# Three PSUM banks for the gates and the inverse root's tiny operations spread between mixing and candidate, in a two-layer graph network kernel

## What is computed

```python
h = jnp.maximum(_layernorm(x, axis=-1), 0.0)
x = x + _L0_gnn_ref(h, ...)          # messages, segment_sum, then the GRU update:
#   r = sigmoid(i_r + h_r);  z = sigmoid(i_z + h_z)
#   n = tanh(i_n + r * h_n); new = (1 - z) * n + z * h
h = jnp.maximum(_layernorm(x, axis=-1), 0.0)
x = x + _L1_gnn_ref(h, edge_index, edge_attr_16, ...)
#   starts from projections of h: h @ W_att1 (source and target parts)
```

## Time and profile before

| | |
|---|---|
| median of 3 runs | 7310.7 us (7306.98 to 7316.62) |
| profiled execution, its own time | 7319.67 us |
| its span | 7317.9 us |
| update of layer 0 within it | 2479 to 2741 us |
| busy over the span: TensorE, VectorE, ScalarE, GpSimd | 77%, 61%, 29%, 68% |

### The profile page before, as it was taken

One profiled execution on the slowest core, in us unless ns is written; L12 is line 12 of the kernel. 1 busy time (PEld: TensorE's weight loads), 2 busy tenths in 40 slices (PEclk: granted clock), 3 DMA queues, 4 the chain that ended last, 5 costly groups with the idle time before them and its releaser, 6 DMA issues.

```text
span 7317.9 us, 186920 instructions
## 1 busy us (share of the span) xinstructions
PE 5607.2 (77%) x34843; PEld 4551.4 (62%) x34844; DVE 4494.2 (61%) x19972; ACT 2133.7 (29%) x6161; POOL 5006.6 (68%) x10349
## 2 busy tenths in 40 slices
PE   5555777878655767888788888886888888888885
PEld 2345555555555547777777777775767666666773
DVE  3466777777433663333333333333999999999997
ACT  3111100000000242222222222222555555555553
POOL 0377777777777356777777777776777777777771
PEclk8755565555555686666666656666898999999889
DMA  7223322222322123333333333333333333333332
GB/s 218 76 57 59 59 57 56 58 57 56 57 58 58 41 80 127 106 107 107 103 102 102 103 101 102 102 102 131 91 95 94 95 95 94 94 95 94 94 91 72
DMA packets 1128092, 649.01 MB, mean 89 GB/s; under 512 B 782033, under 2 KB 1031683, under 8 KB 1127044
## 3 DMA queue, kind: packets, MB, share of 16 engines
q1 hardware_dynamic: 766708, 357.79, 19.4%
q0 software_dynamic: 137728, 233.30, 10.5%
q10 hardware_dynamic: 223584, 57.12, 3.4%
HBM read 360.62 MB, written 311.42 MB: 92 GB/s over the span
## 4 chain that ended last, share of the span: by engine, by line
PE 20%; issue 16%; POOL 11%; DVE 9%; ACT 2%; DMA 2%; DVEq 1%; POOLq 1%; ACTq 0%; SPq 0%
PE banks L1287 9%; PE banks L1289 6%; POOL rows_by_src L779 4%; DVE h L1836 2%; PE banks L1334 2%; DMA rows_by_src<-ring 2%; PE banks L1288 2%; DVE h L1841 1%; DVE ring L1847 1%; PE banks L1275 1%; ACT ring L995 1%; POOL ring L840 1%; POOL ring L824 1%; DVE acc L1832 1%; POOL ring L821 1%
## 5 line engine op out<-in xcount | busy, mean ns | idle before, releaser
L779 POOL DMA_INDIRECT rows_by_src<-ring x1760 | 1779.5, 1011 | 563.7 <-issue 496.1
L751 POOL DMA_INDIRECT wide<-msg_table,ring x1664 | 1629.6, 979 | 761.9 <-issue 451.9
L1287 PE MATMUL banks<-wide,ring 128*128 x3520 | 1240.3, 450 | 271.5 <-ACT ring L988 183.3
L1287 PEld LDWEIGHTS banks<-wide,ring 128*128 128x128 f32 x3520 | 818.1, 286 | 352.0 <-issue 349.8
L1289 PE MATMUL banks<-h,ring 128*128 x3520 | 964.6, 371 | 0.0
L1289 PEld LDWEIGHTS banks<-h,ring 128*128 128x128 f32 x3520 | 837.2, 292 | 123.1
L995 ACT COPY ring<-banks 128x416 f32<-128x416 f32 x880 | 402.3, 510 | 1651.2 <-PE banks L1289 1651.2
L1204 PE MATMUL banks<-wide,ring 128*128 x3520 | 813.9, 412 | 66.1 <-DVE ring L1683 64.2
L1204 PEld LDWEIGHTS banks<-wide,ring 128*128 128x128 f32 x3520 | 779.9, 323 | 127.2 <-issue 123.2
L1804 DVE COPY ring<-ring 128x4 f32<-128x4 f32 x440 | 80.4, 183 | 1229.6 <-DMA rows_by_src<-ring 1229.4
L1169 PE MATMUL banks<-ident,ring 128*128 128x128 f32 x1248 | 421.1, 467 | 534.7 <-ACT ring L926 289.0
(11 more groups left out here) (317 smaller groups left out, 10757.3 us busy)
## 6 DMA issues: line engine op xcount, KB each, us to landing
h<-rows_by_src SPq DMA_DIRECT2D x1776, 105.0 KB, 2.0
ring<-attr_turned SPq DMA_DIRECT2D x440, 128.0 KB, 2.3
attr_turned<-ring ACTq DMA_DIRECT2D x416, 96.0 KB
rows_by_src<-ring POOLq DMA_INDIRECT x1760, 2.5
wide<-msg_table,ring POOLq DMA_INDIRECT x1664
msg_table<-ring SPq DMA_DIRECT2D x100, 256.0 KB, 2.0
ring<-attr_by_dst SPq DMA_DIRECT2D x208, 64.0 KB
attr_turned<-ring ACTq DMA_DIRECT2D x208, 64.0 KB
```

Source lines behind the costliest of these rows:

```text
L751: g.indirect_dma_start(out=A_g[:, b * GV + u, :], out_offset=None, in_=table[:, :], in_offset=bass.IndirectOffsetOnAxis(ap=A_idx[:, s, u:u ...
L779: g.indirect_dma_start(out=rows_d[:, :], out_offset=bass.IndirectOffsetOnAxis(ap=B_pos[:, s, u:u + 1], axis=0), in_=B_row[:, s, u, :], in_ ...
L1287: mm(b[:, 0:H1], B_DT[:, t, u, :], q_tab[:, w, :].rearrange("p a k -> p (a k)"), start=True, stop=False)
```

## The change

- The gates of pair j go to bank 2, 3 or 7 in turn (`G_BANK`), and TensorE waits for the sum of pair j-3 instead of j-2. Bank 7 is not used by anything else in this stage. `G_t` keeps two buffers, with ScalarE's wait on them.
- The inverse root of group g no longer stands in one block in slot 5g+8. Its twelve operations are called one at a time by `root(k, n_of_slot)`, six in slot 5g+9 and six in slot 5g+10: one behind each of the four operations of mixing and adding and the two of the candidate. Each waits for its own predecessor by `s_std`, which now counts operations. A dependent operation of mixing waits for its predecessor (`ch.need`) behind the tiny one.
- The deviation (5g+6), the square (5g+7) and the sum of squares (5g+8) keep their slots. The scaling moves from slot 5g+9 to 5g+11, which is the slot of the next group's deviation, and stands behind it. `G_LAG` grows from 11 to 13 and `G_STORE` with it: all that follows the scaling (TensorE's turns and products, ScalarE's copies, GpSimd's parts, SP's stores) comes two slots later.

The number of instructions is the same on every engine.

```diff
--- before.py
+++ after.py
@@ -79,8 +79,9 @@
 AT_SQRT, AT_FLAG, AT_COUNTS, AT_SORT, AT_TURN, AT_BOUND = 7, 13, 16, 19, (22, 24), (27, 30, 32)
 G_GROUP = 5
 N_GROUPS = NW // 2 // G_GROUP
-G_NORM = (G_GROUP + 1, G_GROUP + 2, G_GROUP + 3, G_GROUP + 4)
-G_LAG = 2 * G_GROUP + 1
+G_DEV, G_SQ, G_VAR, G_ROOT, G_SCALE = (G_GROUP + n for n in (1, 2, 3, 4, 6))
+G_LAG = 2 * G_GROUP + 3
+G_BANK = (2, 3, 7)
 G_SLOTS = NW // 2 + G_LAG + 2
 G_STORE = G_LAG + 5
 RSQRT_BITS = 0x5f3759df
@@ -951,13 +952,13 @@
                     act.wait_ge(g_mm, j + 1)
                     if j >= 2:
                         act.wait_ge(g_x, j - 1)
-                    a.activation(G_t[:, j % 2, :, :], two(bank[2 + j % 2], 4 * HID)[:, :, HID:GATES], ACT.Tanh, scale=0.5).then_inc(g_t, 1)
+                    a.activation(G_t[:, j % 2, :, :], two(bank[G_BANK[j % 3]], 4 * HID)[:, :, HID:GATES], ACT.Tanh, scale=0.5).then_inc(g_t, 1)
                 if k == T + 1:
                     act.wait_ge(r_pos, R_STEP * RANK_LOOPS)
                     a.copy(recs1[:, :, 0], src_T).then_inc(r_c, 1)
                     a.copy(recs1[:, :, 1], place_T).then_inc(r_c, 1)
                     act.wait_ge(r_c, 2 * REC0)
-                g, step = divmod(k - G_NORM[1], G_GROUP)
+                g, step = divmod(k - G_SQ, G_GROUP)
                 if 0 <= g < N_GROUPS and step == 0:
                     act.wait_ge(s_dev, g + 1)
                     if g >= 2:
@@ -1238,10 +1239,10 @@
                 if 0 <= j < T:
                     pe.wait_ge(g_Tc, j + 1)
                     pe.wait_ge(c_in[j % H_SLOTS], X_LOADS[j % H_SLOTS] + 16 * (j // H_SLOTS + 1))
-                    if j >= 2:
-                        pe.wait_ge(g_x, j - 1)
+                    if j >= 3:
+                        pe.wait_ge(g_x, j - 2)
                     for u in range(2):
-                        b = bank[2 + j % 2][:, u * 4 * HID:(u + 1) * 4 * HID]
+                        b = bank[G_BANK[j % 3]][:, u * 4 * HID:(u + 1) * 4 * HID]
                         mm(b, ones_b[:, :], bias3[:, 0:BIAS0], start=True, stop=False)
                         last = mm(b, h0m[:, j % H_SLOTS, u, :], wst0[:, :], start=False, stop=True)
                     last.then_inc(g_mm, 1)
@@ -1735,47 +1736,83 @@
             for t in P_hT:
                 v.memset(t[HID:HID + 1, :, :], 1.0).then_inc(p_ones, 1)
 
-            def norm_group(g, step):
-
-                n = 2 * G_GROUP
+            n = 2 * G_GROUP
+
+            def of_group(g):
                 w = slice(g * n, (g + 1) * n)
-                var, std, total = (small[:, j * NW + w.start:j * NW + w.stop] for j in range(3))
+                return (w,) + tuple(small[:, j * NW + w.start:j * NW + w.stop] for j in range(3))
+
+            def spread(g):
+
+                w, _, _, total = of_group(g)
+                dve.wait_ge(g_x, (g + 1) * G_GROUP)
+                ch.link(v.tensor_reduce(total, xs[:, w, :], AX.X, ALU.add))
+                v.scalar_tensor_tensor(h[:, w, :], per_row(total, n), -1.0 / HID, xs[:, w, :], ALU.mult, ALU.add).then_inc(s_dev, 1)
+
+            def root(k, n_of_slot):
+
+                g, late = divmod(k - G_ROOT, G_GROUP)
+                if not (0 <= g < N_GROUPS and late < 2):
+                    return
+                _, var, std, t = of_group(g)
+                step = 6 * late + n_of_slot
+                dve.wait_ge(s_std, 2 + 12 * g + step) if step else dve.wait_ge(s_var, 2 + g + 1)
                 if step == 0:
-                    ch.link(v.tensor_reduce(total, xs[:, w, :], AX.X, ALU.add))
-                    v.scalar_tensor_tensor(h[:, w, :], per_row(total, n), -1.0 / HID, xs[:, w, :], ALU.mult, ALU.add).then_inc(s_dev, 1)
-                if step == 2:
-                    dve.wait_ge(s_sq, g + 1)
-                    v.tensor_reduce(var, G_sq[:, g % 2, :, :], AX.X, ALU.add).then_inc(s_var, 1)
-                    dve.wait_ge(s_var, 2 + g + 1)
-                    ch.link(v.tensor_scalar(var, var, 1.0 / HID, EPS, ALU.mult, ALU.add))
-                    ch.link(v.tensor_scalar(std.bitcast(i32), var.bitcast(i32), 1, None, ALU.arith_shift_right))
-                    ch.link(v.tensor_scalar(std.bitcast(i32), std.bitcast(i32), -1.0, float(RSQRT_BITS), ALU.mult, ALU.add))
-                    for turn_no in range(3):
-                        ch.link(v.scalar_tensor_tensor(total, std, -0.5, var, ALU.mult, ALU.mult))
-                        ch.link(v.tensor_tensor(total, total, std, ALU.mult))
-                        m = v.scalar_tensor_tensor(std, total, 1.5, std, ALU.add, ALU.mult)
-                        if turn_no < 2:
-                            ch.link(m)
-                    m.then_inc(s_std, 1)
-                if step == 3:
-                    dve.wait_ge(s_std, 2 + g + 1)
-                    v.scalar_tensor_tensor(h[:, w, :], h[:, w, :], 0.0, per_row(std, n), ALU.max, ALU.mult).then_inc(s_h, 1)
+                    m = v.tensor_scalar(var, var, 1.0 / HID, EPS, ALU.mult, ALU.add)
+                elif step == 1:
+                    m = v.tensor_scalar(std.bitcast(i32), var.bitcast(i32), 1, None, ALU.arith_shift_right)
+                elif step == 2:
+                    m = v.tensor_scalar(std.bitcast(i32), std.bitcast(i32), -1.0, float(RSQRT_BITS), ALU.mult, ALU.add)
+                elif step % 3 == 0:
+                    m = v.scalar_tensor_tensor(t, std, -0.5, var, ALU.mult, ALU.mult)
+                elif step % 3 == 1:
+                    m = v.tensor_tensor(t, t, std, ALU.mult)
+                else:
+                    m = v.scalar_tensor_tensor(std, t, 1.5, std, ALU.add, ALU.mult)
+                m.then_inc(s_std, 1)
 
             T = NW // 2
             for k in range(G_SLOTS):
-                if 1 <= k < T + 1:
-                    j = k - 1
-                    w = slice(2 * j, 2 * j + 2)
-                    mix(j // G_PAIRS, j % G_PAIRS, h[:, w, :], g_n)
-                    v.tensor_tensor(xs[:, w, :], xs[:, w, :], G_d[:, j % 2, :, :], ALU.add).then_inc(g_x, 1)
+                j = k - 1
+                w, old, d, e = slice(2 * j, 2 * j + 2), G_n[:, j % 2, :, :], G_d[:, j % 2, :, :], G_e[:, j % 2, :, :]
+                if 0 <= j < T:
+                    dve.wait_ge(g_n, j + 1)
+                    m = ch.do(v.tensor_tensor(d, h[:, w, :], old, ALU.subtract))
+                root(k, 0)
+                if 0 <= j < T:
+                    ch.need(m)
+                    m = ch.do(v.scalar_tensor_tensor(e, G_t[:, j % 2, :, HID:2 * HID], 1.0, d, ALU.add, ALU.mult))
+                root(k, 1)
+                if 0 <= j < T:
+                    ch.need(m)
+                    m = ch.do(v.scalar_tensor_tensor(d, e, 0.5, old, ALU.mult, ALU.add))
+                root(k, 2)
+                if 0 <= j < T:
+                    ch.need(m)
+                    v.tensor_tensor(xs[:, w, :], xs[:, w, :], d, ALU.add).then_inc(g_x, 1)
+                root(k, 3)
                 if k < T:
-                    candidate(k // G_PAIRS, k % G_PAIRS, two(bank[2 + k % 2], 4 * HID), g_t, g_v)
-                for step, lag in enumerate(G_NORM):
-                    g, rest = divmod(k - lag, G_GROUP)
-                    if 0 <= g < N_GROUPS and rest == 0:
-                        if step == 0:
-                            dve.wait_ge(g_x, (g + 1) * G_GROUP)
-                        norm_group(g, step)
+                    gates, u = two(bank[G_BANK[k % 3]], 4 * HID), G_u[:, k % 2, :, :]
+                    dve.wait_ge(g_t, k + 1)
+                    m = ch.do(v.scalar_tensor_tensor(u, G_t[:, k % 2, :, 0:HID], 1.0, gates[:, :, GATES:4 * HID], ALU.add, ALU.mult))
+                root(k, 4)
+                if k < T:
+                    ch.need(m)
+                    v.scalar_tensor_tensor(G_v[:, k % 2, :, :], u, 0.5, gates[:, :, 0:HID], ALU.mult, ALU.add).then_inc(g_v, 1)
+                root(k, 5)
+                g, rest = divmod(k - G_DEV, G_GROUP)
+                if 0 <= g < N_GROUPS and rest == 0:
+                    spread(g)
+                g, rest = divmod(k - G_VAR, G_GROUP)
+                if 0 <= g < N_GROUPS and rest == 0:
+                    dve.wait_ge(s_sq, g + 1)
+                    v.tensor_reduce(of_group(g)[1], G_sq[:, g % 2, :, :], AX.X, ALU.add).then_inc(s_var, 1)
+                g, rest = divmod(k - G_SCALE, G_GROUP)
+                if 0 <= g < N_GROUPS and rest == 0:
+                    w, _, std, _ = of_group(g)
+                    dve.wait_ge(s_std, 2 + 12 * (g + 1))
+                    v.scalar_tensor_tensor(h[:, w, :], h[:, w, :], 0.0, per_row(std, n), ALU.max, ALU.mult).then_inc(s_h, 1)
+
 
             dve.wait_ge(r_c, 2 * REC0)
             v.memset(B_row[:, :, :, ROW_ONE:ROW], 1.0).then_inc(b_pad, 1)
```

## The result

The changed kernel took 7274.77 us (median of five, 7271.24 to 7281.26), the kernel before beside it 7311.99 us (five, 7306.98 to 7318.92): 0.9948 times, 95% interval 0.9934 to 0.9961. That is 38 us less by the ratio, 28 to 48. The forecast was 7278.6, within 7263 to 7298. A second series gave 7274.31 against 7310.41, 0.995 (0.9936 to 0.9964).

The account below looks back on a forecast made before the run. No engine was full: VectorE, TensorE and ScalarE waited in a ring in layer 0's update. Terms of -4.6 us per steady group made -37.4 in all, +5.4 for the lag, net -32: 7278.6 us, range 7263 to 7298.

Parts of the forecast that it names:

- The block (-4.03): VectorE, layer 0's update: the twelve tiny operations no longer stand in a row, saving 4.03 us per steady group.
- its return (+1.0): Tiny operations spread over two VectorE slots beside GpSimd still cost 1.0 us per group, bounds 0.2 to 1.9.
- Rival 2: VectorE: nothing hides the spread tiny operations, 3.2 us per group instead of 1.0; kernel 7296 us; chance 0.12.
- The wait behind the scaling (-2.1): VectorE's wait for the candidate's tanh shrinks from 2.47 us (1.84 to 2.78) to 0.38 per group.
- the tanh wait that the scaling had hidden (+0.38): VectorE: moving the scaling saves 0.73 us per group but uncovers a tanh wait of 0.38.
- Mixing beside GpSimd (+1.3): GpSimd's chain falls on VectorE mixings formerly free of it: +1.0 us in one slot, +0.3 in another, per group.
- The third bank (-0.4 a group): TensorE makes gates one slot earlier, so VectorE's 0.46 us wait for the gates' tanh goes: -0.4 on average.
- Rival 4: TensorE follows ScalarE's copies, so the third bank does nothing: 3 us less gain, 7282 us; inside the forecast, no own chance.
- Rival 1: VectorE's tanh wait is only half the block's consequence; the 2.1 us stays; -24 us in all, 7286; chance 0.15.
- Rival 3: GpSimd holds each tiny VectorE operation, 0.55 us on average; kernel slower by 24 us, 7335; chance 0.03.
- The wait behind the deviation stays, as does TensorE's slow stretch there: VectorE's 2.37 us wait behind each group's deviation, and TensorE's slow stretch there, stay, since deviation, square and copies keep slots.
- The signs: Idle expected afterwards: TensorE's ahead of the gates under 25 us; VectorE's ahead of mixing under 35, 0.4 in four slots of five.

Follow-up runs that it names:

- Run 4: The changed kernel without nine of each group's twelve tiny operations (the three turns left out): stage 216.9 us instead of 224.9, 8468.19 us on a slower chip.
- run 3: The kernel before without nine of the twelve tiny operations in each group's block: stage 224.9 us instead of 260.4, 8484.66 us on a slower chip.
- run 1: The kernel before with the third bank alone, the inverse root still a block: stage 253.7 us, 8504.7 against 8516.82 on a slower chip, 0.9984.
- run 2: The changed kernel with two banks and the old wait: stage 229.0 us, 8489.71 against 8516.82 for the kernel before on a slower chip, 0.9962.
- run 6: The changed kernel with ScalarE's square one slot later: stage 224.0 us, 7276.77 us, 0.9954 of the kernel before.
- run 9: The changed kernel with the square a slot later behind that slot's copies, and the scaling ahead of the deviation: stage 201.8 us, 7256.18 against 7313.46, 0.9921.
- run 11: The changed kernel with the square at the end of slot 5g+8, scaling left behind the deviation, lag 14: stage 206.5 us, 7258.9 us, 0.9923.

## Why the prediction was right, point by point

- **The mechanism and the sum**: -32 us forecast in the stage, -35.5 measured (-35.8 between the second profiles of each). Per steady group 20.4 forecast, 20.1 measured; the first -2.9 against -3.2, the last -2.4 against -2.3, the lag +5.4 against +4.7. The group from the second to the third deviation gave -5.6 instead of -4.6. GpSimd's chains begin two slots later in the changed kernel, so this group is free of their holds for longer: of its 18.8 us 10 lie beside them, before 21 of 24.4. That was not in the sum.
- **The block (-4.03) and its return (+1.0)**: right in size, -3.95 and +1.15 on average. The two slots with tiny operations and GpSimd took 2.53 and 2.51 us from L1780 to L1797, where the earlier trace rows have 2.19 beside GpSimd, and 1.27 from candidate to mixing, 0.98 without them: some 1.2 a group. Run 4 says 0.8 to 1.0 for nine.
- **Rival 2**, that nothing hides the tiny ones, fell. At 2590.46 to 2590.90 the dependent big operations start 0.33 us apart, each with a tiny one between, which is what they take without (0.32 by the same count). The Trainium skill, "VectorE: DVE Perf Modes", section "The DRAIN you can't avoid", has the next operation wait for an empty pipe, and adds that one which is not held starts earlier. The trace agrees with the second part, which the prediction left out: L1769 starts 0.21 us after L1784, which lasts 0.29. Runs 3 and 4 price the same nine at 35.5 and 8.0 us.
- **The wait behind the scaling (-2.1)** and **the tanh wait that the scaling had hidden (+0.38)**: right, and the cause of the first too, by run 3, and by run 1 not the bank. The wait was 2.58 on average in the six steady groups. Both terms leave 0.38 of a wait; no wait is seen there (2589.73, 2593.50), because the tiny operations fill that time: 1.27 and 1.26 us from candidate to mixing, and 0.98 without them in the second slot, 0.38 of it the wait. From candidate to mixing the fourth slot lost 0.28 by that count and the fifth 2.20, forecast 0.35 and 2.1.
- **Mixing beside GpSimd (+1.3)**: this term was too large. By the table mixing takes 1.1 us more a group; some 0.6 of it are the tiny operations' (2.45 and 2.51 where 2.19 stands without them), so 0.5 are GpSimd's. The third and the fourth slot came further beside its chain, as forecast, but the fifth got free of it (2593.50 to 2594.68, 1.18 us, 2.19 before). The prediction did not take that off.
- **A wait that the sum did not have**: in the slot of the first tiny operations, where the block had covered it, mixing waits for the tanh, 0.37 us at 2585.93, 0 to 0.71 in the six groups, 0.29 on average. The measured terms are then -3.95 + 1.15 - 0.28 - 0.38 - 2.20 + 0.53 + 0.29 = -4.84 (block, tiny ones, scaling, bank, wait, mixing, new wait), for -4.03 + 1.0 - 0.35 - 0.4 - 2.1 + 1.3 = -4.6 (-0.35 is -0.73 + 0.38). Two misses partly cancel.
- **The third bank (-0.4 a group)**: 4.1 us in the stage by run 2, 0.4 a group. Rival 4, that it does nothing, is wrong. Without it TensorE waits up to 1.46 us for the sum in a steady group. That the bank is what ended the wait of 0.46 is shown by run 1 for the kernel before; run 3 ended it without the bank.
- **Rival 1** (the wait stays) would have had 21.5 us a group or more; 20.1 measured. **Rival 3** (GpSimd's holds) would have had tiny operations above 400 ns on average: only L1771 does, 409; the whole stage is 35.5 us shorter.
- **"The wait behind the deviation stays, as does TensorE's slow stretch there"**: right, 1.64 us plus the scaling's 0.73, and the granted clock of 0.50 behind it. What the prediction did not see is that this wait has two causes, and that the new place of the scaling added the second.
- **The signs**: TensorE's idle ahead of the gates (6.4 for under 25) and VectorE's ahead of mixing (24.0 for under 35) came as said, but two of the four small waits of 0.4 are not there. The upper bound of the last wait was taken too wide: seven times 2.78 less 2.47 is 2.2, not 4.
- **The whole kernel**: 7274.8 against 7278.6. The medians lie 37.2 apart, 35.5 of it is the stage, and the other 1.7 are within the spread of the runs.

## What to carry to other kernels

A chain of tiny dependent operations costs its length times what waits for its end; put one by one between the dependent operations of the engine's main work, it cost 8 us here instead of 35.5. When such a wait is gone, look for the one behind it in the engines that share an in-order queue: here the square ahead of the copies, and the scaling ahead of the transposes, each of which hid the other. Moving the square by a slot, or behind its slot's copies, gave nothing; the scaling ahead of the deviation cost 5 us; the square moved by both, with either way past the scaling, gave 23 and 18.

## What the runs showed that was not expected

- Among VectorE's operations the reductions L1749 and L1809 (810 and 812 ns) and the candidate's L1797 and L1801, which read PSUM (277 and 282 ns), keep their length beside GpSimd, while mixing's three between SBUF tiles run at 511, 367 and 477 ns on average and reach 0.81, where 0.29 is free. The tiny ones reach 0.69, where 0.15 is free.
- The slow product behind a stand of TensorE is its clock. Behind the stands of 4.4 to 4.7 us in the steady groups of the changed kernel and of run 6, L1263 takes 2.13 to 2.26 us instead of 1.14 to 1.21, under a granted clock of 0.50. Other stands went either way: one of 1.88 us in the kernel before is followed by 2.26 us (2592.47), in run 9 those of 2.04 by 1.14 and those of 2.55 to 3.26 by 2.13, from group to group in turn, and in run 11 those of 1.0 to 1.6 by 1.14 to 1.21, all in steady groups. ScalarE's copy waits for that product (1.55 us in run 6), so such a stand costs more than its own length.
